# Attention units of eight batches in one straight sequence, with each projection issued in one go beneath one unit in four

## The reference, cut to what matters

```python
Q = (layernorm(x) @ Wq + bq); K = ctx @ Wk + bk; V = ctx @ Wv + bv      # 16 heads of 32
attn = softmax(Q_h @ K_h.T / sqrt(32), axis=-1)                          # per head, 512 x 512
x1 = x + concat_h(attn @ V_h) @ Wo + bo
xn1 = layernorm(x1)
logits = einsum('bntd,des->bntes', grouped(xn1), Wc) + bc + tie          # 32 tokens a group
perm = (logits == max over the group's tokens)
```

## Time and profile before

| | |
|---|---|
| median of 3 runs | 2713.75 us (2713.5 to 2720.8) |
| profiled execution, its own time | 2702.48 us |
| its span, first to last instruction | 2700.7 us |
| mean granted TensorE clock | 0.904 |
| first to last exponential of the attention phase | 54.98 to 1208.16 us |
| busy in the span | PE 83%, DVE 54%, ACT 52%, POOL 14% |

### The profile page before, as it was taken

The page is one execution under the profiler, slowest core; times in us unless marked ns, Lnnn a source line. Parts: engine busy times, 40 slices in busy tenths (PEclk is TensorE's granted clock), DMA queues, the critical chain, the costliest instruction groups (busy, mean ns, idle before and its releaser), DMA issues. The chain is left out here.

```text
span 2700.7 us, 45348 instructions
## 1 busy us (share of the span) xinstructions
PE 2241.2 (83%) x14571; PEld 1408.1 (52%) x14571; DVE 1458.7 (54%) x2518; ACT 1407.4 (52%) x3038; POOL 364.9 (14%) x513
## 2 busy tenths in 40 slices
PE   7988989898998988985986974779798988979766
PEld 4645556464655556563845731545454544545442
DVE  2746556473746556471342331476757666675764
ACT  3736456473746547470332332667565565756553
POOL 0000000000000000001201200313213131321320
PEclk9999999999999999997998996588797888979787
DMA  5333232323223232224567567522212221321100
GB/s 156 103 95 92 66 109 64 111 74 114 64 75 104 67 113 69 81 53 117 137 223 209 172 215 261 208 100 102 95 62 87 65 90 59 116 97 55 43 20 16
DMA packets 196450, 280.61 MB, mean 104 GB/s; under 512 B 29280, under 2 KB 91776, under 8 KB 191040
## 3 DMA queue, kind: packets, MB, share of 16 engines
q1 hardware_dynamic: 166880, 250.69, 30.6%
q10 hardware_dynamic: 29408, 27.80, 3.4%
HBM read 148.23 MB, written 63.05 MB: 78 GB/s over the span
## 5 line engine op out<-in xcount | busy, mean ns | idle before, releaser
L449 ACT ACTIVATE a_prob<-a_score,a_negmax 128x512 f32<-128x512 f32 x512 | 354.0, 693 | 275.5 <-DVE a_negmax L521 232.1
L521 DVE TENSOR_REDUCE a_negmax<-a_score 128x1 f32<-128x512 f32 x512 | 342.5, 684 | 142.9 <-PE a_score L683 137.6
L690 PE MATMUL a_turn<-a_ident,a_prob 128*128 128x128 f32 x2048 | 327.4, 284 | 93.9 <-ACT a_probT L309 77.6
L690 PEld LDWEIGHTS a_turn<-a_ident,a_prob 128*128 128x128 f32 x2048 | 237.7, 143 | 232.3 <-ACT a_probT L309 101.8
L309 DVE COPY a_probT<-a_turn 128x512 f32<-128x512 f32 x256 | 176.1, 688 | 155.3 <-PE a_turn L690 154.9
L683 PE MATMUL a_score<-a_k_stack,a_q_stack 128*128 128x512 f32 x512 | 250.1, 491 | 7.6 <-issue 6.8
L1755 PE MATMUL c_work<-c_xT,c_cT 64*128 64x512 f32 (+3 forms) x512 | 179.3, 497 | 38.8 <-DVE c_decay L1523 38.8
L1287 POOL TENSOR_SCALAR c_diag<-c_negm,c_aL 128x128 f32<-128x128 f32 x256 | 165.5, 664 | 339.2 <-issue 118.9
L378 POOL TENSOR_TENSOR a_x<-a_xs,a_bo 128x512 f32<-128x512 f32 x32 | 39.6, 1271 | 1063.5 <-DVEq L588 1012.6
L1768 PE MATMUL c_mix<-c_v,c_decay 128*128 128x65 f32 x1280 | 174.0, 297 | 0.0
L1755 PEld LDWEIGHTS c_work<-c_xT,c_cT 64*128 64x128 f32 x512 | 102.7, 211 | 134.8 <-issue 72.7
(11 more groups left out here) (191 smaller groups left out, 3686.2 us busy)
## 6 DMA issues: line engine op xcount, KB each, us to landing
a_k_stack<-a_k_parts SPq DMA_DIRECT2D x512, 64.0 KB, 2.0
a_q_stack<-a_q_parts SPq DMA_DIRECT2D x512, 64.0 KB, 2.0
scratch_res<-b_res SPq DMA_DIRECT2D x32, 1024.0 KB, 4.7
c_res<-scratch_res SPq DMA_DIRECT2D x32, 1024.0 KB, 9.5
b_xn<-scratch_xn SPq DMA_DIRECT2D x68, 256.0 KB, 2.7
c_hid<-in_L_ffn_W ACTq DMA_DIRECT2D x16, 1024.0 KB, 5.1
c_negm<-scratch_m SPq DMA_DIRECT2D x64, 256.0 KB, 3.7
a_cs<-in_ctx SPq DMA_DIRECT2D x8, 1024.0 KB, 8.0
```

The source lines that it names most:

```text
L449: nc.scalar.activation(prob[:, u % 4, :], score.bank(u)[:, :], ACT.Exp, bias=negmax[:, u:u + 1], accum_out=sums[:, head_of(u), tile_of(u): ...
L521: nc.vector.tensor_reduce(negmax[:, u:u + 1], score.bank(u)[:, :], AX.X, ALU.max, negate=True).then_inc(max_ready, 1)
L690: last = nc.tensor.transpose(turn.bank(u)[:, k * P:(k + 1) * P], prob[:, u % 4, k * P:(k + 1) * P], ident[:, :])
```

## The change: what it does, and the diff

1. The hardware loop is gone: all engines run straight lists over the steps `g` from 0 to 570 (512 units and 59 steps behind them), and units of the next batch follow directly on those of the last.
2. The products are taken from the table `PRODUCTS`: `(first unit, slices per unit, kind, number, batch offset)`. Every entry has 4 slices per unit, so a product is issued in one go beneath one unit. Twelve stand at units 2, 6, ... 46, then L at 48, V at 51, 55, 59 and K1 at 62. O and L are those of the batch before; V, K0, Q0 and K1 are those of the batch after.
3. Turned tiles move from the `work` banks to the two `turn` banks, in the order of the table `TURNS`, and share them with the probabilities.
4. Within step `g` PE's list is `scores(g+2)`, `turn_probs(g-1)`, `mix_values` (for `g` = 2 modulo 4), the product, the tile. DVE's is `maximum(g+1)`, `probs_out(g-1)` for even `g`, then the rest. ACT's is `exponentials(g)`, `probs_out(g-1)` for odd `g`, tiles turned in step `g-1`, products of step `g-1`, then norms and DMA issues. So ACT copies even units out, DVE odd ones, as before.
5. `v` and `attnT` become double; `rwide` and `rsumT` become single; NT is written into `attnT`, and the choice into `logit`. `x` is loaded a second time for the residual. Loads of `x` and `cs` after the first are issued by ACT's queue, and so are the 16 DMAs that stack Q0 of the first batch. K and Q stacks have semaphores of their own.
6. The first Q1 moves from ahead of the first unit to beneath unit 2, and K1 behind the product for `bo`.

```diff
-    own = {11: ("K", 2), 17: ("Q", 2), 18: ("R", 0), 27: ("K", 3), 32: ("Q", 3), 34: ("R", 1), 50: ("R", 2), 66: ("R", 3)}
-    ahead = {34: ("CT", 0), ...
-             46: ("K", 0), 53: ("Q", 0)}
-    STATS_AT, RESULT_AT = 22, 28
+    MIX_AT = HM + 2
+    PRODUCTS = ((2, 4, "Q", 1, 0), (6, 4, "K", 2, 0), (10, 4, "Q", 2, 0), (14, 4, "O", 0, -1), (18, 4, "O", 1, -1),
+                (22, 4, "K", 3, 0), (26, 4, "Q", 3, 0), (30, 4, "O", 2, -1), (34, 4, "O", 3, -1), (38, 4, "V", 0, 1),
+                (42, 4, "K", 0, 1), (46, 4, "Q", 0, 1), (48, 4, "L", 0, -1), (51, 4, "V", 1, 1), (55, 4, "V", 2, 1),
+                (59, 4, "V", 3, 1), (62, 4, "K", 1, 1))
+    TURNS = ((1, "R", 3, -1), (17, "R", 0, 0), (25, "CT", 0, 1), (27, "CT", 1, 1), (29, "CT", 2, 1), (31, "CT", 3, 1),
+             (33, "R", 1, 0), (35, "XT", 0, 1), (37, "XT", 1, 1), (39, "XT", 2, 1), (41, "XT", 3, 1),
+             (43, "NT", 0, -1), (45, "NT", 1, -1), (46, "NT", 2, -1), (47, "NT", 3, -1), (49, "R", 2, 0), (54, "PM", 0, -1))
+    STATS_AT, SCALE_AT, RESULT_AT = 14, 20, 21
+    CHOICE_AT, PERM_AT = 51, 57
+    STEPS = ALL + PERM_AT + 2
...
-            with eng.Fori(0, B - 1) as b:
-                body(b, b * ROUNDS + BASE0, TURN, True)
-            body(B - 1, (B - 1) * ROUNDS + BASE0, LAST, False)
...
     ScalarE
+                stack_parts(act, "Q", 0)
+                act.dma_start(cs[:, :, :], tiled(A["ctx_1024"])[1]).then_inc(c_in, 16)
+                for t in range(T):
+                    product_out("V", 0, t)
+                for g in range(STEPS):
+                    b, u = divmod(g, UNITS)
+                    if g < ALL:
+                        exponentials(g)
+                    if 1 <= g <= ALL and g % 2 == 1:
+                        probs_out(nc.scalar.copy, act, g - 1)
+                    if g > 0:
+                        for job in turn_at[g - 1]:
+                            turned(*job)
+                    for job in product_ended[g - 1]:
+                        product_out(*job)
...
+                    if u == STATS_AT + T + 1 and b + 1 < B:
+                        norm0.on_scalar(act, b + 1)
+                    if u == 33 and b + 2 < B:
+                        act.dma_start(cs[:, :, :], tiled(A["ctx_1024"])[b + 2]).then_inc(c_in, 16)
+                    if u == 39 and b >= 1:
+                        norm1.on_scalar(act, b - 1)
...
     VectorE
+                for g in range(STEPS):
+                    b, u = divmod(g, UNITS)
+                    if g + 1 < ALL:
+                        maximum(g + 1)
+                    if 1 <= g <= ALL and g % 2 == 0:
+                        probs_out(nc.vector.tensor_copy, dve, g - 1)
+                    if g > 0:
+                        for job in product_ended[g - 2]:
+                            if job[0] in ("K", "Q"):
+                                low(*job)
+                    if g % UG == 0 and UG <= g <= ALL:
+                        widen(g // UG - 1)
+                    if g % UG == MIX_AT - 2 and UG < g <= ALL + MIX_AT:
+                        scale_mixed(g // UG - 1)
+                    for job in product_ended[g - 1]:
+                        if job[0] == "O":
+                            last = add_residual(*job[1:])
...
     TensorE
+                product("K", 0, 1, range(C))
+                for U in range(AHEAD):
+                    scores(U)
+                for g in range(STEPS):
+                    if g + AHEAD < ALL:
+                        scores(g + AHEAD)
+                    if 1 <= g <= ALL:
+                        turn_probs(g - 1)
+                    q, rest = divmod(g - MIX_AT, HM)
+                    if rest == 0 and 0 <= q < ALL // HM:
+                        mix_values(q)
+                    for kind, b, n, steps in product_at[g]:
+                        product(kind, b, n, steps)
+                    for job in turn_at[g]:
+                        turn_tiles(*job)
```

More of the change, by code:

```diff
@@ L240, in attention_phase @@
+    product_ended[-1].append(("K", 0, 1))
     with ctx:
@@ L296, in turns, with wait_stack @@
[L296 to L309 removed]
+        def wait_stack(eng, kind, M):
+            eng.wait_ge(stack_in[kind][M % 2], STACKED * (M // 2 + 1))
@@ new lines, in stack_parts @@
+        def stack_parts(eng, kind, M):
+            b, m = divmod(M, GROUPS)
+            if M >= 2:
+                score.wait_full(eng, 0, (M - 1) * UG - 1)
+            work.wait_read(eng, 0, jobs[kind, b, m])
+            for i, part in enumerate({"K": KEY_PARTS, "Q": QUERY_PARTS}[kind]):
+                for g in range(HM):
+                    eng.dma_start(stack[kind][i * DH0:(i + 1) * DH0, M % 2, g, :].bitcast(F32),
+                                  parts[kind][g * DH0:(g + 1) * DH0, part, :].bitcast(F32)).then_inc(stack_in[kind][M % 2], 16)
@@ L444, in exponentials @@
-                def exponentials(b, u):
-                    act.wait_ge(max_ready, b * UNITS + (u + 1))
-                    if u >= 4:
-                        turn.wait_full(act, b, u - 4)
-                    nc.scalar.activation(prob[:, u % 4, :], score.bank(u)[:, :], ACT.Exp, bias=negmax[:, u:u + 1],
-                                         accum_out=sums[:, head_of(u), tile_of(u):tile_of(u) + 1]).then_inc(score.free[u % 3], 1)
-                for u in range(AHEAD):
-                    exponentials(0, u)
@@ L486, in _, with exponentials @@
-                turns(act, body)
+                def exponentials(U):
+                    act.wait_ge(max_ready, U + 1)
+                    if U >= 4:
+                        turn.wait_full(act, 0, entries["P", U - 4])
+                    u = U % UNITS
+                    nc.scalar.activation(prob[:, U % 4, :], score.bank(U)[:, :], ACT.Exp, bias=negmax[:, u:u + 1],
+                                         accum_out=sums[:, head_of(U), tile_of(U):tile_of(U) + 1]).then_inc(score.free[U % 3], 1)
@@ L612, in _, with scores @@
                 pe.wait_ge(pool_const, 2)
[L614 to L624 removed]
+                def scores(U):
+                    M, t, g = group_of(U), tile_of(U), U % HM
+                    if U % UG == 0:
+                        wait_stack(pe, "K", M)
+                        pe.sem_inc(pe_parted, 1)
+                        wait_stack(pe, "Q", M)
+                    score.wait_free(pe, 0, U)
+                    nc.tensor.matmul(score.bank(U)[:, :], stack["Q"][:, M % 2, g, t * P:(t + 1) * P], stack["K"][:, M % 2, g, :],
+                                     start=True, stop=True).then_inc(score.full[U % 3], 1)
@@ L710, in _ @@
[L710 to L720 removed]
+                        last.then_inc(work.full[j % 2], 1)
```

672 lines of the change are left out of this document (283 added, 389 removed).

## The result

| kernel | median | runs | against before |
|---|---|---|---|
| before | 2714.16 us | 2713.5 to 2720.8 | |
| after | 2786.57 us | 2779.0 to 2793.2 | 1.026 (95%: 1.0229 to 1.0292) |

The change makes the kernel slower by 72 us. The forecast was slower by 22, with 2790 as the upper end. The profiled execution took 2788.3 us; its span is 2786.6, that of before 2700.7, so here the difference is 86.

What follows compares the result with a forecast made beforehand. PE was taken as the engine nearest its limit, busy 134.0 of 152 us a round. Phase 21, start 0, end -2 and method 3 made +22: 2702.5 to 2724, with 11 for the median 2736 us; range 2640 to 2790.

Steps and rivals of the forecast that it cites:

- The wait behind a product: At the third score behind each product PE waits for an exponential held behind ACT's copy: 0.8 to 1.4 us a group.
- The chain of the bare group: Single steps added up behind a product without tile or norm: 8.75 us for K, Q or V; PE alone 7.34.
- The first rival: PE does not wait behind a product: rounds near 128 us, 2546 us in all, 2640 by half; chance 0.25.
- the second, no change: Nothing measurable changes, the sum being off by 1 to 3% downwards: 2714 us; chance 0.17.
- The last batch: Its units must also carry O0 to O3, L and NT of the batch before: 125.5 us, against 95.0 before.
- my waits are hardly more than half of the one seen: Argument against a clock fall: PE's 3 to 4 us behind norms, against 6.17 us at the loop turn.
- The rival: The clock falls behind both norms' waits: 16 stretches cost 3 us each, 2784 us in all; chance 0.08.
- The two norm groups: Groups behind O1 and V0, where table loads shift exponential g+2 by 2.9 us: forecast 11.0 and 12.3 us.
- The method's shortfall: Adding up steps fell short by 0.14 us on a group with no product; 3 us added for it.
- The start: Ahead of the first unit, Q1 goes but Q0's 16 DMAs delay V0's evacuation: first score at 54, between -3 and +3.
- The median: The median of the runs lies 11 us above the profiled execution, taking the forecast from 2724 to 2736.
- The stacks: On SP's queue, 16 DMAs take 11.2 us each, 90 a round of 153: hidden, Q1 and Q2 having least room.

Runs made afterwards that it cites:

- The lists reordered: After with norms at units 18 and 38, plus exponential g+2 ahead of the copy of g and the evacuation behind exponential g+3: 2663.9 us.
- slices: After with products in single slices beneath each of four units, L and K1 in two halves: 2619.8 us, 0.967 of before.
- parity: After with the products at units 2 to 46 one unit later, L at 49, still in one go: 2679.9 us, 0.9905 of before.
- halves: After with two slices beneath each of two units for every product: 2703.5 us; with norms at 18 and 38 as well: 2681.7 us.

## Why the prediction was right in sign and wrong in size

*The wait behind a product: right in mechanism, near in size.* The chain of the bare group was met to 0.01 us in its first three steps, and 0.14 short at its end. The lists reordered show it alone; slices, parity and the old kernel with products in one go agree, though the clock has a share in the first two. PE's waits ahead of scores are 15.2 us in five of the six rounds, where I said some 20, and 7.2 of them stand behind the two norms. The first rival, that PE does not wait, is dead: rounds are 158.5 to 163.7 and not below 150. So is the second, no change: the ratio is 1.026, 1.0229 at the least.

*The last batch: right.* 129.8 for 125.5, and 95.0 before. These 35 us are nearly half of what the phase lost, and the forecast had them from the work that the unbroken sequence puts beneath the last batch's units. No run separates that work.

*The step that failed: "Against it: my waits are hardly more than half of the one seen."* With it I gave the clock 0.08 and put it into the sum at nothing. The waits of 3 to 4 us that I had worked out were there (3.71 and 3.47), and the clock fell behind 13 of 14. I had read the one wait of the earlier trace rows as a bound, and the trace of before already spoke against that, in two places. Its pause of 6.17 us ended at 210.85 and so began at 204.68, and the clock was 0.50 from 207.00 on the earlier trace rows: it fell 2.3 us after PE had stopped, not after 6.17. And one of its norms, behind a pause no longer than the one of the earlier trace rows, had a fall too, which the prediction does not mention:

```profile
710.68 0.66 PE L690 MATMUL a_turn<-a_ident,a_prob 128*128 128x128 f32 x4 [1.59 <-ACT a_prob L449]
...
712.20:715.60 3.40, 3.40 (x26) 1.75 (x28) 2.67 (x5) 2.78 (x8) 0.00 (x0) 0.50 0.10 24
```

The first is a row of the timeline, the second one of the windows view. The other six norms beneath units of before, with pauses of 1.58 or 1.59 us, had none.

The rival was right in kind. Its price was 3 us for each of 16 stretches; a fall in the K3 group cost 1.6 to 2.7, and there are 14 norms beneath units, not 16. The two norm groups are 2.1 and 2.0 us over the forecast on the mean of the rounds, 25 of the 44 us by which the six rounds missed. Moving the norms by one unit took 62 us away, wait and clock together. That this rival's 2784 lies 3 us from the measured 2786.6 is luck: as far as the groups tell, the clock gave little more than half of its 48 us, and the start, the shortfall and the phases behind the rest.

*The method's shortfall: 3 us credited, some 16 met.* All groups without a norm are 0.1 to 0.2 us longer than their chains, L with V1 and the eleven units behind V1 0.5 to 0.6 each, together 2.6 in round 3 and so 16 in six rounds. The 0.14 by which the method had fallen short on one group, taken for each of the 102 groups of six rounds, would have been 14; I added 3 for everything. The last 3 of the 44 us are the Q2 group of round 5.

*The start: "between -3 and +3", measured +9.2.* I had the 16 DMAs ahead of V0's evacuation right (45.22, directly behind them) and called them hidden. What I had not counted are two more issues that the change gives to ACT: the first `x` and `Wq` now stand, with the six small loads that it had before, ahead of its first copy, at 16.76 instead of 10.29. Point 5 of the change does not name them either. How the 13.6 us of the start divide between these two loads and the 16 DMAs was not measured.

*The median.* Before's profile lay 11 us below its median and I added that to the forecast; after's lies 2 above. That is 13 us between the miss of the profiled execution (64) and that of the medians (51).

*The stacks.* SP's queue was hidden in after, as forecast, but for the one wait of 1.59 us in round 5. It came out as soon as groups were shorter: 31 us of waits with halves.

## What to carry to other kernels

When engines work through fixed lists, a long job on one of them costs as much as stands, in another's list, behind the first entry that needs its end: cut the job into slices, or put ahead of that entry all that could run during it. Do the chain for the groups with extra work too, since one held entry pushes all of them. And a pause worked out at 3 us is a price in itself and may bring a second one, the clock. One long pause with a fall does not say that a shorter one has none: look at when in the pause the clock fell, and at every fall in the trace. Put table loads beneath a job of the matmul engine that is longer than they are.

## What the runs showed of the hardware

- The granted clock fell to 0.50 behind pauses of PE much shorter than the loop turn's 6.17 us: 4.77 us in the halves with moved norms, 3.71 and 2.96 in after, 1.59 once in before. In the kernel with reordered lists it fell behind a wait of 1.92 us, ahead of an R tile:

```profile
512.95 0.93 PE L660 MATMUL a_turn<-a_ident,a_rwide 128*128 128x128 f32 x4 [1.92 <-DVE a_rwide L507]
```

  It fell there in five of six rounds at the same unit, and in the sixth, behind 1.91 us, it did not. That O1 group took 11.5 us in the five rounds and 9.95 in the sixth, so a fall there cost 1.6. The waits of 1.26 us, one in each bare group of after's round 3, had no fall behind them. Such a stretch lasted 3.4 or 6.8 us in the records, and once 10.2, in the old kernel with products in one go.
- Issuing a stack of 16 DMAs held ACT for 10.56 us and SP for 11.15, and on ACT that was time in which nothing else of its list ran: it was idle for 12.05 us ahead of its next copy.
- Two table loads with a square root between them cost PE 2.8 us where it waits for the exponential behind them (K3 group 11.29 without a fall, 8.49 with the norm moved), and nothing that can be seen where they lie beneath a product of 3.44.
